# State-space layers with three decay banks, one read-out for both channel tiles, and norms moved inside the layers

## The reference, cut to what matters

```python
xi, z = split(x @ in_proj)                       # 256 channels each
u = silu(causal_conv(xi, 4 taps) + conv_b)
dtr, Bc, Cc = split(u @ x_proj)                  # 64, 16, 16
delta = softplus(dtr @ dt_proj + dt_b)           # (time, 256)
A = -exp(A_log)                                  # (256, 16)
def step(h, inp):                                # over 512 time steps
    d_t, b_t, c_t, u_t = inp
    h = exp(d_t[:, :, None] * A) * h + (d_t * u_t)[:, :, None] * b_t[:, None, :]
    return h, einsum('bdn,bn->bd', h, c_t)
y = (scan(step) + u * D) * silu(z)
out = y @ out_proj
```

```python
ft = sigmoid(xt @ wf.T + c @ uf.T + bf); it = sigmoid(xt @ wi.T + c @ ui.T + bi)
gt = tanh(xt @ wc.T + c @ uc.T + bc);    c = ft * c + it * gt
h = tanh(x @ wo.T + c_final @ uo.T + bo)
```

## Time and profile before

| | us |
|---|---|
| median of 3 runs | 2786.44 (2774.48 to 2787.81) |
| the profiled execution | 2772.27, span 2770.5 |
| busy in the span | TensorE 2350.1, VectorE 1764.9, ScalarE 1270.1, POOL 645.6 |
| layer 10, from 1747.3 | first scan 1772.7, last finish ends 2058.5 |
| layer 14, from 2407.9 | first scan 2437.6, last finish ends 2721.8 |
| norm in front of layer 11 | 2059.1 to 2073.0 |
| norm in front of layer 15 | 2722.4 to 2734.8 |

### The profile page before, as it was taken

How to read it: one execution, slowest core, us unless ns; L and a number is a source line. 1 busy time by engine, 2 the same in 40 slices (tenths; PEclk the granted TensorE clock), 3 DMA queues, 4 the chain that set the end, 5 groups by cost and what they waited for, 6 DMA issues and landing times. The chain is left out here.

```text
span 2770.5 us, 30672 instructions
## 1 busy us (share of the span) xinstructions
PE 2350.1 (85%) x9760; PEld 1000.2 (36%) x9760; DVE 1764.9 (64%) x2747; ACT 1270.1 (46%) x2497; POOL 645.6 (23%) x740
## 2 busy tenths in 40 slices
PE   8999999677399989779987799688779989877878
PEld 3333334322122234454553344223234456322323
DVE  5666665577877645543545645589874547478895
ACT  3555653178277731312423253455645412265563
POOL 1111110322111100211010100356640032155661
PEclk9999999878699989988679899899899989989889
DMA  3000000122000020000000000000000000000000
GB/s 149 1 1 1 1 1 1 21 41 32 2 1 1 1 92 0 1 1 1 1 1 0 0 1 0 0 1 0 0 0 1 1 1 2 1 0 1 0 0 16
DMA packets 9358, 25.92 MB, mean 9 GB/s; under 512 B 1072, under 2 KB 7280, under 8 KB 8176
## 3 DMA queue, kind: packets, MB, share of 16 engines
q1 hardware_dynamic: 8336, 23.18, 3.0%
q10 hardware_dynamic: 864, 0.79, 0.2%
HBM read 16.56 MB, written 1.05 MB: 6 GB/s over the span
## 5 line engine op out<-in xcount | busy, mean ns | idle before, releaser
L3272 PE MATMUL l_py<-l_read,w_const 128*128 128x512 f32 x512 | 315.2, 702 | 93.4 <-DVE l_read L3405 74.7
L3549 POOL TENSOR_TENSOR l_drive<-l_du,l_bsb 128x512 f32<-128x512 f32 x256 | 325.9, 1297 | 206.2 <-ACT l_bsb L3346 187.0
L3396 DVE TENSOR_TENSOR_SCAN l_state<-l_decay,l_drive 128x512 f32<-128x512 f32 x256 | 310.4, 1213 | 57.9 <-ACT l_decay L3354 50.4
L402 ACT ACTIVATE l_probs<-l_psp,l_stats 128x512 f32<-128x512 f32 x256 | 172.9, 682 | 150.6 <-DVE l_stats L412 150.6
L3354 ACT ACTIVATE l_decay<-l_delta,l_a 128x512 f32<-128x512 f32 x256 | 176.4, 689 | 138.0 <-DVE l_state L3396 137.6
L263 POOL TENSOR_TENSOR l_nx_small<-l_nx_small,w_const 128x4 f32<-128x4 f32 x38 | 40.4, 1063 | 777.3 <-DVE l_nx_small L257 777.3
L3272 PEld LDWEIGHTS l_py<-l_read,w_const 128*128 128x128 f32 x512 | 99.1, 214 | 248.0 <-DVE l_read L3405 207.4
L1278 DVE TENSOR_REDUCE l_tops<-l_ring 128x2 f32<-128x1024 f32 x128 | 151.5, 1220 | 44.9 <-PE l_ring L1269 44.5
L410 DVE TENSOR_REDUCE l_stats<-l_psp 128x2 f32<-128x1024 f32 x128 | 156.2, 1220 | 35.8 <-PE l_psp L364 35.1
L3405 DVE TENSOR_TENSOR l_read<-l_state,l_pc 128x512 f32<-128x512 f32 x256 | 168.3, 657 | 0.0
L718 DVE SCALAR_TENSOR_TENSOR l_product<-l_psu,w_gated,l_first 128x512 f32<-128x512 f32 x104 | 78.0, 750 | 137.8 <-ACT l_first L692 137.5
(11 more groups left out here) (561 smaller groups left out, 4435.2 us busy)
## 6 DMA issues: line engine op xcount, KB each, us to landing
l_stack<-l_parts SPq DMA_DIRECT2D x84, 64.0 KB
w_gated<-in_gated SPq DMA_DIRECT2D x1, 3297.5 KB, 12.0
w_mha<-in_mha SPq DMA_DIRECT2D x1, 2568.5 KB, 13.4
w_ssm<-in_ssm SPq DMA_DIRECT2D x2, 1171.0 KB, 16.0
w_moe<-in_moe SPq DMA_DIRECT2D x1, 2248.0 KB, 18.3
w_const<-in_const SPq DMA_DIRECT2D x1, 1325.0 KB, 7.7
x<-x_in SPq DMA_DIRECT2D x1, 1024.0 KB, 4.9
out<-x SPq DMA_DIRECT2D x1, 1024.0 KB, 3.9
```

Source lines behind the costliest of these rows:

```text
L402: act.activation(probs[:, s % 4, i, :], psp[:, s % 2, i, :], ACT.Exp, bias=stats[:, s % 4, 1, i:i + 1], scale=scale, accum_out=stats[:, s ...
L3272: pe.matmul(py[:, t, :], eye, read[:, s % 4, :], start=n == 0, stop=n == NS - 1, skip_group_check=True)\
L3396: dve.tensor_tensor_scan(state[:, s % 4, :], decay[:, s % 2, :], drive[:, s % 4, :], 0.0, ALU.mult, ALU.add).then_inc(L["state"].sem, 1)
L3549: pool.tensor_tensor(drive[:, s % 4, :], du[:, b % 2, t, :], bsb[:, n % 2, :], ALU.mult)\
```

## The change

In `state_space`:

- The loop goes over 64 pairs k = (batch, state). VectorE does the two scans of a pair, then one read-out of both tiles of the pair before, 1024 columns, against one bank of C. `state` and `read` have two buffers of a pair, `drive` and `bsb` three (`RING`); POOL writes one drive of 1024 columns a pair.
- `decay` has three PSUM banks, `pc` one.
- The skip term is a matmul with a diagonal matrix of D into the sum's bank (`add_skip`), before the first `add_up` of a batch; the gate reads the sum from PSUM. In batches after the first it waits for the gate of the batch before.
- The positive part is a Relu on ScalarE for batches 1 to 3 (batch 0: VectorE, as before).
- z is projected one batch earlier, at n = 14 and 15; for batch 0 before the loop, with its Silu. `u` and `du` have one buffer in place of two. The second tile's Silu reads PSUM directly.
- The split moves from n = 10 to n = 8, the positions of other steps move by one or two.
- The norms of batches 0, 1 and 2 for the next layer stand in the last batch's loop (`nx`), and layer 10 normalises the last batch of its own input in its batch 0 (`late`).
- The taps (weights of the convolution) are made in two instructions; the Exp of `a_log` and the first `copy_b` move behind the first soft_exp.

In the tuples, layers 10 and 14 now normalise the next layer's input, and layers 10, 11 and 15 take the last batch inside. The section in front of layers 11 and 15 goes, that in front of 14 stays.

```diff
-def state_space(nc, core, name, g):
-    ST = NS * CT
+def state_space(nc, core, name, g, inner, last_in):
+    PAIRS = B * NS
+    RING = 3
...
-        bsb = L.sb("bsb", [P, 2, S])
-        drive, state, read = (L.sb(n, [P, 4, S]) for n in ("drive", "state", "read"))
+        bsb = L.sb("bsb", [P, RING, S])
+        drive = L.sb("drive", [P, RING, CT, S])
+        state, read = (L.sb(n, [P, 2, CT, S]) for n in ("state", "read"))
...
-        decay, pc, py = (L.ps(n, [P, 2, S]) for n in ("decay", "pc", "py"))
-        pb, front = L.ps("pb", [P, S]), L.ps("front", [P, S])
+        decay, py = L.ps("decay", [P, RING, S]), L.ps("py", [P, CT, S])
+        pc, pb, front = (L.ps(n, [P, S]) for n in ("pc", "pb", "front"))
...
+        def add_skip(pe, b, t):
+            if b:
+                pe.wait_ge(L["gated"].sem, L["gated"].at(b - 1, t + 1))
+            else:
+                pe.wait_ge(L["skip_diag"].sem, L["skip_diag"].at(0, t + 1))
+            pe.matmul(py[:, t, :], skip_diag[:, t, :], u[:, t, :], start=True, stop=False, skip_group_check=True)
+
+        def add_up(pe, k):
+            pe.wait_ge(L["read"].sem, L["read"].at(0, k + 1))
+            for t in range(CT):
+                mm = pe.matmul(py[:, t, :], eye, read[:, k % 2, t, :], start=False, stop=k % NS == NS - 1,
+                               skip_group_check=True)
+            mm.then_inc(L["summed"].sem, 1)
...
+        def decays(act, k, t):
+            b, n = divmod(k, NS)
+            s = k * CT + t
...
+            if s >= RING:
+                act.wait_ge(L["state"].sem, L["state"].at(0, s - RING + 1))
...
+        def read_out(dve, k):
+            dve.wait_ge(L["state"].sem, L["state"].at(0, CT * (k + 1)))
+            dve.wait_ge(L["rows_c"].sem, L["rows_c"].at(0, k + 1))
+            if k >= 2:
+                dve.wait_ge(L["summed"].sem, L["summed"].at(0, k - 1))
+            dve.tensor_tensor(read[:, k % 2, :, :], state[:, k % 2, :, :],
+                              pc[:, :].unsqueeze(1).to_broadcast([P, CT, S]), ALU.mult).then_inc(L["read"].sem, 1)
...
+                for k in range(PAIRS):                      # TensorE
+                    b, n = divmod(k, NS)
+                    if k + 1 < PAIRS:
+                        spread_c(pe, k + 1)                 # waits for read k + 1
+                    if b and n == 0:
+                        for t in range(CT):
+                            add_skip(pe, b, t)
+                    add_up(pe, k)
+                    if k + 4 < PAIRS:
+                        spread_b(pe, k + 4)
+                    between(pe, b, n)
...
+                for k in range(PAIRS):                      # ScalarE
+                    decays(act, k, 0)
+                    if k + 1 < PAIRS:
+                        copy_b(act, k + 1)
+                    decays(act, k, 1)
+                    if n in (1, 2) and b:
+                        raw_z(act, b, n - 1)
+                    if ahead:
+                        if n == 3:
+                            raw_x(act, b + 1)
+                        if n == 6:
+                            for t in range(CT):
+                                silu_x(act, b + 1, t)
+                        if n == 8:
+                            copy_low(act, b + 1)
+                        if n in (9, 11):
+                            magnitude(act, b + 1, (n - 9) // 2)
+                            positive_part(act, b + 1, (n - 9) // 2)
+                        if n == 11:
+                            for t in range(CT):
+                                soft_exp(act, b + 1, t)
+                        if n == 12:
+                            for t in range(CT):
+                                soft_log(act, b + 1, t)
+                        if n == 13 and b == 0 and last_in:
+                            late.square(act, B - 1)
+                    if n == 6 and b:
+                        for t in range(CT):
+                            silu_z(act, b, t)
+                    if not ahead and n in (4, 10, 14):
+                        nx.square(act, (n - 4) // 5)
...
+                for k in range(PAIRS):                      # VectorE
+                    for t in range(CT):
+                        scan(dve, k, t)
+                    if k:
+                        read_out(dve, k - 1)
+                    if b and n == 1:
+                        gate(dve, b - 1)
+                    if b + 1 < B:
+                        if n == 8:
+                            split_parts(dve, b + 1)
+                        if n in (12, 13):
+                            add_positive(dve, b + 1, n - 12)
...
+                    else:                                   # last batch
+                        if n == 4:
+                            nx.keep(dve, 0)
...
+                        if n == 8:
+                            finish(dve, b - 1)
...
+                read_out(dve, PAIRS - 1)
+                nx.diag(dve, 2)
+                nx.scale(dve, 2)
                 gate(dve, B - 1)
                 finish(dve, B - 1)
...
-NORMALISES_NEXT = (0, 1, 2, 3, 4, 5, 6, 7, 8, 9, 11, 12)
-NORMALISES_LAST = (1, 2, 3, 4, 5, 6, 7, 8, 9, 11, 12, 13)
+NORMALISES_NEXT = (0, 1, 2, 3, 4, 5, 6, 7, 8, 9, 10, 11, 12, 14)
+NORMALISES_LAST = (1, 2, 3, 4, 5, 6, 7, 8, 9, 10, 11, 12, 13, 15)
```

More of the change, by code:

```diff
@@ L3176, in state_space @@
+        decay, py = L.ps("decay", [P, RING, S]), L.ps("py", [P, CT, S])
+        pc, pb, front = (L.ps(n, [P, S]) for n in ("pc", "pb", "front"))
+        kept, square = L.sb("kept", [P, 1, S]), L.sb("square", [P, S])
+        nx = NextNorm(L, front[:, :], buffers=(kept, square, square[:, :].rearrange("p (t q) -> p t q", q=P)))
+        late = NextNorm(L, front[:, :], last=True, shared=nx)
         eye = core.w("const", "eye")
         def x_bank(b, t):
-            return pc[:, 0, :] if b == 0 and t == 1 else front[:, :]
+            return decay[:, 0, :] if b == 0 and t == 1 else front[:, :]
@@ L3182, in pre_bank @@
         def pre_bank(b, t):
[L3184 to L3199 removed]
+            return decay[:, 0, :] if b == 0 and t == 0 else front[:, :]
@@ new lines, in z_bank, with project_z @@
+        def z_bank(b, t):
+            return front[:, :] if b else decay[:, 1 + t, :]
+        def project_z(pe, b, t):
+            if b and t == 0:
+                pe.wait_ge(L["soft_abs"].sem, L["soft_abs"].at(b, CT))
+                pe.wait_ge(L["soft_pos"].sem, L["soft_pos"].at(b, CT))
+            if b == 1 and t == 0 and last_in:
+                pe.wait_ge(L["in_xn"].sem, L["in_xn"].at(0, 1))
+            if b >= 2 and t == 0:
+                pe.wait_ge(L["done"].sem, L["done"].at(b - 2, 1))
+            if b and t:
+                pe.wait_ge(L["zraw"].sem, L["zraw"].at(b - 1, t))
+            if b == B - 1 and last_in:
+                pe.wait_ge(L["in_xn"].sem, L["in_xn"].at(0, 1))
+            pe.matmul(z_bank(b, t), w("w_in", DI + t * P, DI + (t + 1) * P), core.normed(b), start=True, stop=True)\
+                .then_inc(L["zps"].sem, 1)
@@ new lines, in _ @@
+                for t in range(CT):
+                    dve.tensor_scalar(skip_diag[:, t, :], eye, w("skip", t, t + 1), None, ALU.mult)\
+                        .then_inc(L["skip_diag"].sem, 1)
+                split_parts(dve, 0)
+                for t in range(CT):
+                    dve.wait_ge(L["soft_abs"].sem, L["soft_abs"].at(0, t + 1))
+                    dve.tensor_scalar(positive[:, t, :], pre_bank(0, t), w("dt_b", t, t + 1), 0.0, ALU.add, ALU.max)\
+                        .then_inc(L["soft_pos"].sem, 1)
```

440 lines of the change are left out of this document (222 added, 218 removed).

## The result

The changed kernel takes 2800.4 us, the kernel before 2779.7 (medians of 15 runs each on the same chips): a ratio of 1.0081, 95% interval 1.0066 to 1.0096, by that ratio 22 us slower. The forecast was 2782, some 4 us under the 2786.4 that stood for the kernel before (a median of 3 runs; the 15 give 2779.7), and no change that can be told. The measured time lies inside the stated range of 2753 to 2804, but near its upper end and on the other side of the kernel before; a slower kernel had been given 16%. The profiled execution of the changed kernel has a span of 2798.0 us, 27.5 more than the one before.

What follows compares the result with a forecast made beforehand. VectorE was taken to set the pace, with slack on TensorE. Layer 14 was to lose 9.7 us, layer 10 13.4, and the seams to gain 27.1: -4.0 on 2786.4, so 2782 us, range 2753 to 2804.

Steps and rivals of the forecast that it cites:

- (a): ScalarE's copy of the convolution at pair 3 waits for TensorE: VectorE waits 3.6 us in batches 1 and 2.
- (d): Second delta, TensorE's step 9, ends 6.7 us into pair 10, so pair 12 starts 3.0 us late.
- (e): Ln block with two table loads makes VectorE wait 1.6 us, before 1.22.
- the finish in the last batch: Finish of batch 2 at pair 8 waits 4.2 us for its projection, with all scans queued behind it.
- Rival 3: TensorE falls to half clock and sets the pace: 2842 us with half the pairs, 2822 with a third; 13%.
- Rival 4: A pair costs 3.50 us, so joining the read-out brings nothing: 2796 us; 11%.
- the sum of VectorE's work: Per state-space layer, 10.9 us gained from pairs and work leaving VectorE, 4.5 added by norms inside the last batch.
- One read-out for both tiles: Scan loop: joint read-out of 1024 columns makes a pair 3.39 us instead of 3.42, 1.9 us gained a layer.
- the waits: VectorE's waits in one state-space layer: 38.5 us, 35.9 at full TensorE clock to 42.2, against 25.3 before.
- (c): The split, moved to pair 8, waits there 1.4 us for the low-rank copy.
- (b): Silu block on ScalarE, which held VectorE 5.72 us, now leaves a wait of 1.2 (0 in batch 0).
- the square of norm 1: Last batch: norm 1, centred by TensorE, squared by ScalarE, kept by VectorE within two pairs, waits 0.6 us.

Runs made afterwards that it cites:

- e3: Kernel before, with every scan also waiting for the read-out directly in front of it: 1.0090 of the kernel before; first to last scan 288.4 and 286.6 us.
- e4: Changed kernel with the norms at seams 9/10, 10/11 and 14/15 standing alone again: 1.0170 of the kernel before; first to last scan 295.4 and 296.4 us.
- e5: Changed kernel with the split moved on VectorE from pair 8 to pair 11: first to last scan 293.3 and 289.1 us, against 300.0 and 300.7.
- e1: Changed kernel with a third state buffer, scan waiting for the read-out before the last: 1.0121 of the kernel before; first to last scan 302.6 and 300.7 us.
- e2: Changed kernel with three state buffers but the old wait for the read-out directly in front kept: 1.0083 of the kernel before.
- e8: Changed kernel with positive parts back on VectorE (pairs 9 and 11): first to last scan 304.8 in layer 10, 297.4 in layer 14, against 300.0 and 300.7.

## Why the prediction was wrong

Right, by its steps: the seams (8.4 for 8.2 at 9/10), start and tail; the read-out's duration, 1.20 for 1.18; wait (a) 3.34 for 3.6; (d) 2.57 to 3.35 for 3.0; (e) 1.51 for 1.6; the finish in the last batch 4.14 for 4.2; TensorE's granted clock over layer 14, 0.88, well above 0.8. Rival 3 did not come. Rival 4, the nearest, has the pair at 3.50, but by scans 1.22 apart and not by a wait; they stand 1.14 apart. No rival names the rest.

The step that failed is the sum of VectorE's work, -10.9 + 4.5 = -6.4 us a layer. In layer 14 first to last scan grew by 25.4, of which 45.8 - 26.8 = 19.0 are waits, so VectorE's own time grew by 6.4: 12.8 us off. Two parts of it are in the rows:
- *One read-out for both tiles.* The pair was to cost 3.39 and costs 3.58. I took the overlap of 0.08 from instructions that wait for nothing (the rows are a read-out and the scan behind it, not two read-outs, as one sentence there has it), and did not see that halving the state's buffers makes the scan wait for the read-out just in front. 31 pairs of layer 14 start so: 31 x 0.21 = 6.5 us.
- *POOL's one product for two tiles.* The cast of the split was to take its 1.37 and takes 2.60, and the six additions in the loop of layer 14 take 9.3 us for 5.9: 3 x 1.23 + 3.4 = 7.1 us. I had priced the longer product nowhere.

They add up to 13.6 us, 0.8 more than is missing. So this step fails by two terms of its sum: the pair (3.39 taken, 3.58 measured) and VectorE's work beside POOL's longer product, put at nothing.

The second step is the waits, 38.5 taken, 45.8 measured in layer 14, outside the upper bound of 42.2: the low-rank copy (c) 2.7 to 2.9 for 1.4 where TensorE was at half clock, the Silus (b) 2.02 for 1.2, the square of norm 1 2.02 for 0.6, and three of 0.8 before the second scan of pairs 0 and 11, named nowhere.

Behind both stands a model of the loop that is too simple, and the experiments show it rather than the sums. I charged work taken off VectorE at its full duration and added waits to it. But a batch is a sequence of round trips (TensorE's step, ScalarE's copy and decay, VectorE's scan). VectorE's work within one can be free: the 6.5 us a layer that the third state buffer took off came back as waits, all of them in layer 14 and more in layer 10, and positives put back shortened layer 14. It is not always so: of the 38 us added in e3 24 counted, and what e4 and e5 took off VectorE shortened the layer by at least as much. Which of the two holds would hang on whether a wait follows in the same round trip; that is argued and not shown. What counts besides is when TensorE's step starts. I had seen that (3.5 us into the next pair) and used it to price each wait, but compared the sum with nothing: the same walk with a read-out per tile might have shown the joint one to be the expensive half of the change. With the positions mended it is 14.5 us a layer lost. I carried it as 1.9 gained, and laid the 13 us of added waits to the change as a whole.

The Trainium skill (VectorE: DVE Perf Modes, the TRN2 errata section) has operations from SBUF pay a fixed latency for each instruction, so that merging should save it. None of these runs bears that out for this product, one operand of which is in PSUM: with no wait for the instruction in front, a pair took 3.36 joined and 2 x 1.71 = 3.42 apart, 0.06 in favour of joining, not the 0.16 estimated from the skill's 150 cycles. The Trainium skill (VectorE: DVE Perf Modes, section "The DRAIN you can't avoid") found, for eight copies, that a semaphore after each costs nothing extra. For a scan behind a read-out e1, e2 and e3 disagree, with 0.21 us wherever the wait is for the operation just in front.

## What to carry to other kernels

Before merging two instructions, ask who is released by the first one: here the merge saved 0.06 us a pair on its engine and cost 14.5 us a layer in waits, because another engine's chain starts at its end. Where an engine shows waits, its own work in front of them may be free (e1, and e8 in layer 14) or may not (e3, e4): try it before counting on it. When moving an instruction changes the time, look also at what now runs beside it on another engine: a good part of what the split's move brought (e5) was its cast getting clear of POOL's product. When buffers are halved, look whether an instruction now waits for the one directly in front of it on the same engine.

## What the runs showed of the hardware

- A scan on VectorE that waits by semaphore for the read-out just in front starts 0.21 us later than one that waits for an older one: 1.32 to 1.11 behind a read-out of 1024 columns, 0.79 to 0.58 behind one of 512.
- A cast and an addition between SBUF operands on VectorE last until the POOL product beside them is over (2.60 and 2.42 us for 0.41 and 0.69 of work, POOL's taking 2.35); read-outs and scans, each with one operand in PSUM, are not held (1.20 and 1.21 on average over the whole kernel, beside 128 such products). The Trainium skill (GPSIMD Engine Reference, Key points) names VectorE instructions in a 2-port mode or with two SBUF inputs as contending with GpSimd for SBUF. The addition has two such inputs, and its rows agree; that the cast ran in a 2-port mode no run here shows. The rows give the price: up to the whole length of the product.
- The same step of TensorE after the same idle time of 2.58 us ran at full clock in one batch and at 0.55 in another.
